# One 288-column product in every expert group, and seven spare products ahead of the first expert rows

## The reference

```python
# T = 4096 tokens, E = 8 experts, K = 2, cap = 1280 rows for one expert
xe = zeros((E, cap + 1, D)).at[experts, pos_safe].set(xf[tokens])[:, :cap]
h = silu(einsum('ecd,edf->ecf', xe, W1)) * einsum('ecd,edf->ecf', xe, W3)
ye = einsum('ecf,efd->ecd', h, W2)
out = zeros((T, D)).at[tokens].add(wk[:, None] * ye[experts, pos])
```

## Time and profile before

| quantity | value |
|---|---|
| median of 3 runs | 1398.87 us |
| lowest, highest | 1397.52 us, 1402.39 us |
| profiled execution, its own time | 1398.93 us |
| its span, first to last instruction | 1397.2 us |
| outside the span (1398.93 - 1397.2) | 1.7 us |
| TensorE busy | 1299.0 us, 93% of the span |
| mean granted TensorE clock | 0.969 of full speed |

### The profile page before, as it was taken

One profiled execution on the slowest core, in us unless ns is written; L12 is line 12 of the kernel. 1 busy time (PEld: TensorE's weight loads), 2 busy tenths in 40 slices (PEclk: granted clock), 3 DMA queues, 4 the chain that ended last, 5 costly groups with the idle time before them and its releaser, 6 DMA issues.

```text
span 1397.2 us, 33423 instructions
## 1 busy us (share of the span) xinstructions
PE 1299.0 (93%) x11085; PEld 1153.5 (83%) x11085; DVE 931.1 (67%) x2770; ACT 640.2 (46%) x1628; POOL 417.4 (30%) x741
## 2 busy tenths in 40 slices
PE   7799999999999999998579999999999999999996
PEld 5577777777777777776369999999999999999996
DVE  5578888888888888887546565565645656565442
ACT  2355555555555555554344344443434435444331
POOL 4114334443444344433302122222221222211112
PEclk9899999999999999997579999999999999999999
DMA  3821210100101010100042242423524334252212
GB/s 96 248 86 34 96 54 25 34 30 30 33 26 34 26 34 25 34 23 24 27 132 31 32 121 32 122 33 48 116 33 113 37 64 94 34 123 32 31 24 24
DMA packets 152459, 80.20 MB, mean 57 GB/s; under 512 B 106210, under 2 KB 145859, under 8 KB 152290
## 3 DMA queue, kind: packets, MB, share of 16 engines
q1 hardware_dynamic: 137698, 59.11, 16.6%
q0 software_dynamic: 14592, 18.91, 7.9%
HBM read 44.04 MB, written 33.96 MB: 56 GB/s over the span
## 4 chain that ended last, share of the span: by engine, by line
PE 80%; DVE 7%; ACT 6%; issue 4%; DMA 1%; POOL 1%; SPq 0%; ACTq 0%; DVEq 0%; POOLq 0%
PE banks L1385 65%; PE banks L1494 4%; PE banks L1379 3%; PE banks L1569 2%; PE banks L1580 2%; PE banks L1489 2%; ACT qk_l L801 1%; ACT qk_e L799 1%; PE banks L1565 1%; DVE r_st L933 1%; DVE hk L1058 1%; DMA xin<-in_x 1%; ACT p_t L721 1%; ACT one_less L811 1%; DVE hv L1059 1%
## 5 line engine op out<-in xcount | busy, mean ns | idle before, releaser
L906 ACT ACTIVATE h_a<-banks 128x256 f32<-128x256 f32 x320 | 122.3, 382 | 348.1 <-PE banks L1385 333.1
L1316 DVE TENSOR_TENSOR h_f<-banks,h_a 128x256 f32<-128x256 f32 x320 | 135.6, 424 | 144.4 <-ACT h_a L906 119.7
L521 POOL TENSOR_TENSOR idle_g<-half 128x1 f32<-128x1 f32 x144 | 32.0, 222 | 533.4 <-DVE y_s L1335 383.0
L1385 PE MATMUL banks<-xe_t_hi,w_even_hi 128*128 128x256 f32 x640 | 180.6, 282 | 3.6 <-issue 2.1
L1385 PE MATMUL banks<-xe_t_hi,w_even_lo 128*128 128x256 f32 x640 | 180.4, 282 | 0.9 <-issue 0.9
L1385 PE MATMUL banks<-xe_t_lo,w_even_hi 128*128 128x256 f32 x640 | 180.4, 282 | 0.0
L1385 PE MATMUL banks<-xe_t_hi,w_odd_hi 128*128 128x256 f32 x640 | 178.2, 279 | 0.0
L1385 PE MATMUL banks<-xe_t_lo,w_odd_hi 128*128 128x256 f32 x640 | 178.2, 278 | 0.0
L1385 PE MATMUL banks<-xe_t_hi,w_odd_lo 128*128 128x256 f32 x640 | 178.2, 278 | 0.0
L895 ACT ACTIVATE h_t_hi<-h_f 128x256 fp32r<-128x256 f32 x320 | 131.7, 412 | 32.6 <-DVE h_f L1316 32.1
L1323 DVE TENSOR_TENSOR h_t_lo<-h_f,h_t_hi 128x256 fp32r<-128x256 f32 x320 | 133.6, 417 | 6.0 <-ACT h_t_hi L895 3.4
(11 more groups left out here) (244 smaller groups left out, 3399.6 us busy)
## 6 DMA issues: line engine op xcount, KB each, us to landing
raw<-in_w SPq DMA_DIRECT2D x24, 1024.0 KB, 5.0
expert_rows<-empty SPq DMA_DIRECT2D x4, 2580.0 KB, 10.9
x_blocks<-expert_rows SPq DMA_DIRECT2D x312, 32.0 KB
xin<-in_x SPq DMA_DIRECT2D x32, 128.0 KB, 2.2
out_dram<-x SPq DMA_DIRECT2D x32, 128.0 KB, 1.7
out_dram<-y_s,token POOLq DMA_INDIRECT x80, 4.0
mask_i<-in_mask SPq DMA_DIRECT2D x32, 32.0 KB, 1.9
expert_rows<-r_xn,send POOLq DMA_INDIRECT x64, 2.6
```

Source lines behind the costliest of these rows:

```text
L521: return pool.tensor_tensor(idle_g[:, i:i + 1], half[:, 0:1], half[:, 0:1], ALU.add)
L906: act.activation(h_a[:, f % 2, :], bank[2 + f % 4][:, 0:GS], ACT.Silu).then_inc(silu_ok, 1)
L1316: dve.tensor_tensor(h_f[:, f % 2, :], bank[2 + f % 4][:, GS:2 * GS], h_a[:, f % 2, :], ALU.mult)\
L1385: last = pe.matmul(dst, lhs, rhs, start=(i == 0), stop=(i == len(pairs) - 1))
```

## The change

It adds a function `fill`, which writes products of the identity and 512 columns of `w_in` (float32) into PSUM bank 2. Nothing reads them. `first_columns` runs four of them at once, waits on TensorE for the four `sent` counts, runs three more, and then waits for `xe` as before. The up products go through a new function, `up_product`, with the same operands in the same order. For the second feature tile (f = 1) of every group the first of the six matmuls of the first up product takes 288 columns instead of 256: 32 columns of the other half of D ride along and are written to columns 256 to 287 of the bank, where the second up product starts afresh later.

```diff
+WIDER = 32
...
+            def fill(times):
+
+                for _ in range(times):
+                    pe.matmul(bank[2][:, :], ident[:, :], w_in[:, 0, 0:2 * D], start=True, stop=True)
+
             def first_columns():
+                fill(4)
+                for i in range(4):
+                    pe.wait_ge(sent[i], 16 * NCH // 2)
+                fill(3)
                 pe.wait_ge(xe_landed, 16)
                 flip(bank[0], [xe[:, 0, a, k * P:(k + 1) * P] for k in range(KT) for a in range(2)], xet_mm)
...
+            def up_product(to, f, m, w, par, more=0):
+
+                both = [t[:, par, :, :].rearrange("p k t -> p (k t)") for t in xe_t]
+                pairs = [(w[m][i][:, k, f * P:(f + 1) * P], both[p], k * GS) for k in range(KT) for i, p in ((0, 0), (0, 1), (1, 0))]
+                for i, (lhs, rhs, at) in enumerate(pairs):
+                    cols = GS + (more if i == 0 else 0)
+                    last = pe.matmul(to[:, m * GS:m * GS + cols], lhs, rhs[:, at:at + cols],
+                                     start=(i == 0), stop=(i == len(pairs) - 1))
+                return last
...
                     to = bank[2 + f % 4]
-                    for m in range(2):
-                        last = split_product(to[:, m * GS:(m + 1) * GS], [
-                            ([w[m][part][:, k, f * P:(f + 1) * P] for part in range(2)],
-                             [xe_t[part][:, par, k, :] for part in range(2)]) for k in range(KT)])
+                    up_product(to, f, 0, w, par, WIDER if f == 1 else 0)
+                    last = up_product(to, f, 1, w, par)
                     last.then_inc(up_mm, 1)
```

## The result

| quantity | before | changed |
|---|---|---|
| median | 1399.79 us (4 runs, 1397.52 to 1402.39) | 1386.16 us (4 runs, 1384.69 to 1387.45) |
| ratio, 95% interval | | 0.9905 (0.9889 to 0.9920) |
| profiled execution, own time | 1398.93 us | 1384.94 us |
| its span | 1397.2 us | 1383.2 us |

The changed kernel is 0.95% faster; two later comparisons gave 0.9902 (0.9885 to 0.9918) and 0.9912 (0.9897 to 0.9927). The forecast was 1394.2 us, and 1392.7 was the low end of its range: the direction was right, the size was too small by 8 us.

The account below looks back on a forecast made before the run. It took TensorE's matmul count times the stream's cost per matmul, plus a few gaps, as the bound: -0.5 - 2.2 + 0.1 + 0.6 - 2.7 = -4.7 us from 1398.93 gives 1394.2 us, range 1392.7 to 1397.9.

Parts of the forecast that it names:

- the pace: Expert stage: TensorE's product stream costs 0.1133 us per product, read from 91 products in 10.31 us.
- The wide products' own cost: Expert groups: 40 products with 32 extra columns add 0.014 us each, +0.6 us; upper end 0.035 each, +1.4.
- The spare products: Between chunks and experts: seven unread products raise the clock; handover +0.1 us, transposes -0.5 us.
- The cover: Before the experts: the last sent rows' landing at 704.53 hides the four products; without it, up to 7.1 us.
- The first products: Start of the experts: 21 products at full clock take 2.4 us in place of 4.59, -2.2 us.
- The transposes rival: Before the experts: transposes do not hold the clock, 21 products run at half clock; 1399.1 us, chance 0.06.
- The jump back: Loop's return: the clock's fall is avoided by a small margin, the second gap stays; -2.7 us.
- the first rival: Loop's jump back: the clock falls all the same; 1396.9 us, or 1395.7 with the second gap gone; chance 0.32.
- the other end of the term: Loop's jump back: 28 more instructions move the jump's target and the second gap goes too; -3.9 us.
- The same stall: Loop's jump back: nothing in the change shortens the stall of 2.13 us, so it stays.
- a fall of the clock in the last group: Behind the last group's 1.8 us wait: a sign of being wrong, 48 products taking 4.3 us more.
- The slow rival: Expert groups: each 288-column product breaks the stream, 0.18 us each, 7.2 us; 1403.5 us, chance 0.05.

Follow-up runs that it names:

- wide_even: Changed kernel with the 288-column product in groups of even number only: 1393.98 us in one run.
- wide8_one32: Changed kernel with 8 extra columns in place of 32, except one product of 32 extra in the second group of all: 1406.60 us in one run.
- Fill_only: Changed kernel with no wide product, the seven spare products kept: 1394.75 us, ratio 0.9964 (0.9953 to 0.9976).
- after_with5: The changed kernel run again, nothing altered, for comparison beside later versions: 1386.31 us.
- wide64_set8: Changed kernel with 64 extra columns in each group's first product instead, and 8 extra in the second group's second tile alone: 1385.01 us in one run.
- wide_f0: Changed kernel with the 32 extra columns in each group's first feature tile in place of the second: 1393.80 us, ratio 0.9960 (0.9944 to 0.9976).
- after_again: The changed kernel run once more, nothing altered, beside later versions: 1385.34 us.
- the two kernels with 64 columns: Changed kernel with 64 extra columns in groups' first products instead: from the third group on, median 1394.76 us; everywhere, plus 32 in every fifth group's second tile, 1394.59 us.
- wide64_reset5: Changed kernel with 64 extra columns in each group's first product instead, plus 32 in every fifth group's second tile: median 1394.59 us, recorded ratio 0.9929.
- wide_f0_64: Changed kernel with 64 extra columns in each group's first product, in place of 32 in the second tile: 1394.73 us in one run.
- results_mid: Kernel before, with the previous group's down products moved into the middle of a group's up products, after the fourth tile: 1399.87 us in one run.
- extra_wait_f4: Kernel before, with one more, already met, TensorE wait ahead of each group's fifth feature tile: 1400.78 us in one run.
- wide8: Changed kernel with 8 extra columns in place of 32 in each group's wide product: 1401.04 us in one run.

## Why the prediction was wrong

**The step that failed is the pace.** The prediction says: "A stretch of the chain of waits gives the pace: 91 products in 10.31 us, 0.1133 us each". That stretch lies in a fast group, and the pace of the other half of the groups is 0.1179 us. Everything that was counted in products was sized from it, and the wide products could then only cost. What they did was to end the slow pace in 18 of the 36 groups that run without a stall: -8.3 us where the sum has +0.5. No rival held that case.

The rows at hand could have shown it. 5760 products at 0.1133 us make 652.6 us. The stalls that the prediction lists add about 2.2 us at the start, 6.0 at the jump back and 2.0 in the last group, 663 in all. The first product starts at 710.01 and the last at 1385.84, 675.8 us. Of the 13 us that are missing, 18 groups x 0.64 us are 11.5, and about half of the rest lies in the last group, which is slow for its first 96 products. I never multiplied the pace by the count.

**The wide products' own cost** was put at 0.014 us with 0.035 as the upper end, and is 0.05 in a fast stream: beyond the range. The product itself is 14 ns longer, its five followers are late as well.

**The spare products**: right. The clock was up 2.9 us after their start, where the sum has 4.4; the transposes took 0.60 us for 1.13; and the wait with the three products behind it cost at most 0.09 us, for the +0.1 of the sum (703.20 to 706.15 is 2.95 us, 704.53 to 707.39 was 2.86). The cover is wide: in wide_even and wide8_one32 the clock rose only near 705.2, over 6 us after the last chunk product, and the first product still came 11.6 and 11.8 us after that one, 11.57 in the changed kernel. Fill_only puts the whole of it, the jump back included, at 0.36%, about 5.0 us; the sum without the wide products was -5.3.

**The first products**: right in kind, -1.7 for -2.2 us. They ran at full clock, but all of group 0 at the slow pace, 11.39 us to the start of group 1. In the profile of after_with5, the same kernel, group 0 is fast, 11.02 us: the pace with which a program's stream sets out differs between its executions.

**The transposes rival** did not come true. The gap of 1.5 us behind them left the clock at 1.00 in every run with the spare products. Whether such transposes count as work, as the Trainium skill denies in TensorE: Matmul & The Clock Gate, Part 4, these runs cannot tell. From the last spare product to the first real one there are 708.24 - 706.15 = 2.1 us, and after stalls of that length at the jump back the clock fell in three traces (2.07 us in wide64_set8 and wide8_one32, 2.11 in the changed kernel) and held in one (2.17, wide_f0).

**The jump back**: -2.2 us for -2.7, by two errors that nearly cancel, which is luck. The clock fell again in the profiled execution, so the first rival was right there, but it was down for 3.4 us where it had been down for 6.8; that is about 1.0 us of the gain. The other 1.2 us are the second gap, which the prediction kept in its sum and which went, in the way that it gave as the other end of the term. "The same stall" was an error too: in the 18 traces it lies between 1.57 and 2.17 us, and the three of the changed kernel have 2.11, 1.65 and 1.89, with the clock fallen, held and fallen. With the spare products ahead, the clock held after all eight stalls up to 1.81 us and fell after four of 1.89 to 2.11; wide_f0, which held after 2.17, shows that the length does not decide it alone.

**Two smaller slips.** With the second gap gone the sum's own terms give 1398.93 - 5.9 = 1393.0 us, not the 1392.7 named as the low end. And a fall of the clock in the last group was priced at 4.3 us; it came in 5 of the 18 traces, not in the changed kernel's own, and cost 1.5 us in after_again (25.81 - 24.28).

**The slow rival**, a wide product that breaks the stream, named the right place, a product of another width in a stream of equals, with the wrong sign.

What stays open: why the stream has these two paces, and what in the return to the up products shifts it. The runs exclude a wait at that place, the buffers of even groups and the instructions themselves, and tie it to the return. Nor is it shown why the two kernels with 64 columns spread over 15 and 31 us; their profiles show one execution each. (The one of 1410.00 us also had a mean granted clock of 0.930, the others of its kernel 0.975 to 0.982.) A kernel whose groups keep the pace would also keep a slow one that an execution set out with or took up at the jump back, and 18 groups at 0.63 us are 11 us: that would do for most of it, but it is argued from wide64_reset5 and wide_f0_64 and no profile shows an execution of 1396 us or more of either kernel.

## What to carry to other kernels

Multiply the pace by the count and compare with the length of the stage before anything is priced with it; an engine that is "100% busy" with equal instructions can still lose 4% in half of its groups, and only the length of one group beside the next shows it. In a long stream of equal matmuls whose group lengths alternate, try one product of another width behind the point where the pace turns, judge it by group lengths and by the spread of several executions, and expect neither the width nor the place to carry over unchanged.

## What the runs showed of the hardware

- A stream of 256-column products with a weight load each runs at 113.3 or 117.9 ns from start to start at full clock, and keeps whichever it has, over more than 2000 products, until something shifts it.
- The return from the down products to the up products shifts it, between 113.3 and 117.9 ns in either direction (results_mid); a met wait does not (extra_wait_f4). A product 8 columns wider can turn it either way (first and later groups of wide8), one 32 columns wider turned it fast or left it as it was. With one 64 columns wider at the shift the groups keep their pace (16.36 or 16.99 us); where there is no shift, in group 1 of wide_f0_64, it turned the stream slow.
- The jump back of the loop costs 1.6 to 2.2 us of stall, not the same in each execution. A second gap of 0.9 to 1.7 us comes after 6, 11 or 13 products, sooner with more code ahead (extra_wait_f4), and is gone with 28 instructions and four waits more.
- The clock can fall at a single idle stretch of 1.9 to 2.1 us between full streams (the changed kernel, after_with5), and behind the wait of 1.8 us in the last group it fell in 5 of the 18 traces.
